# Small-head softmax: scores masked in place in PSUM, exponentials read from there, and their sums in the same banks

## The chip, the cores and the metric

The kernel is one program on one core of a Trainium2 chip. Five engines work side by side, each with its own queue in order: TensorE (PE; its weight loads are shown as PEld), VectorE (DVE), ScalarE (ACT), GpSimd (POOL), and SyncE (SP), which issues DMAs. The metric is the device time of one execution in microseconds; lower is better. PSUM has eight banks of 512 fp32 columns for each of 128 partitions, and matmul results land there.

## What is computed

The model is a stack of layers on x of shape [16, 256, 128] in float32: a mixture of experts, a causal attention with 16 heads of 8 channels, the mixture again, two layers of local attention with gated FFN, a retention layer, and the local layers again. The change lies in the causal attention, which reads in short:

```python
h = _layernorm(x)                       # [16, 256, 128]
q, k, v = split(h @ w_attn + b_attn)    # 16 heads, D = 8
q, k = _rope(q), _rope(k)
att = einsum('bhqd,bhkd->bhqk', q, k) / sqrt(D)
att = where(causal, att, -inf)
att = softmax(att, axis=-1)
y = einsum('bhqk,bhkd->bhqd', att, v)
x = x + y @ w_proj + b_proj
```

## The kernel before

The attention is the stage `small_head_softmax`. A batch is 256 tokens, two tiles t of 128 queries. Queries of tile 0 see 128 keys, those of tile 1 see 256, so one head has 128 + 256 = 384 score columns (`TRI`). A step s handles two heads (h = 0, 1); a batch b has `EACH` = 8 steps, e = 0 to 7, and the stage has U = 16 x 8 = 128 steps. Each head of a step has a PSUM bank of its own, and steps alternate between two pairs: banks 2 and 3 when e is even, 4 and 5 when it is odd.

A step's work goes through the engines like this:
- PE, L936: S, the score matmuls into the pair of banks. L957: transposes of the probabilities of step s-3 into banks 6 and 7. L975, on odd steps: the product with the values for two steps, into bank 1.
- DVE, L1108: four `tensor_tensor_reduce` (t by h). Each reads scores from PSUM, adds the causal mask `tri_q`, writes the masked scores to `pr` in SBUF and the negated row maximum to `nm`. It also reads an accumulator out, a short second row in the trace. L1117: reciprocal of the row sums of step s-1. L1124: copies the transposed probabilities of head 0 from bank 6 to SBUF (step s-3).
- ACT, L1053: four exponentials on `pr`, in place in SBUF, with `nm` as bias; the row sums go to `ls` in SBUF. L1069: the copy of head 1 from bank 7.
- POOL, L1008: multiplies `pr` by the reciprocals.

`pr` has four slots (`SLOTS`), used in turn. Beside this runs the preparation of the next batch: projection and bias (PE L911 at e = 0, ACT L1031), values (PE L918 at e = 4, ACT L1041), rotation on DVE (L1079 `cosines` at e = 1, L1082 `swap` at e = 2, L1086 `sines` at e = 3), its sum on POOL (`total`, L997, at e = 4), `queries` on DVE (L1092, at e = 5, 6, 7 and 0), and POOL's `carry` (L990). ACT L1062 writes the finished batch out at e = 4.

There is no scheduler: the order on each engine is the written order of the loop body, 14 of 16 batches run in a hardware loop of two batches, and the engines meet only at semaphores. Those that matter here: `s_ready` (scores there), `nm_ready` (maxima there), `p_ready` (exponentials done), `rl_ready` (reciprocals done), `normed`, `pt_ready` (transposes done), `pt_low` and `pt_high` (their copies done). S of step s waits for `nm_ready` of s-2, the last reader of its banks.

Of the kernel before, what the change touches and what calls it, by code (L numbers as in the profile page):

```python
# [10 lines left out]
ACT = mybir.ActivationFunctionType  # L11
# [4 lines left out]
B, T = 16, 256  # L16
N = B * T
MASKED = -1e30
FAR = 1e25
# [85 lines left out]
def at_least(u, n):  # L105

    return not isinstance(u, int) or u >= n
# [756 lines left out]
TRI = 384  # L864


def small_head_softmax(nc, g, sem, room, w, tab, bias, prev, room_free):

    U = B * EACH
    SLOTS = 4  # L870
    head_ps, ol = g.bank[0], g.bank[1][:, 0:T]
    s_ps = ((g.bank[2], g.bank[3]), (g.bank[4], g.bank[5]))
    pt_ps = (g.bank[6], g.bank[7])
    hT, xb, turn, qk, qz, vm, nm, ls, rl, pr = (room[x] for x in ("hT", "xb", "turn", "qk", "qz", "vm", "nm", "ls", "rl", "pr"))
    pt = g.z[:, 0:SLOTS * 2 * TRI].rearrange("p (s h n) -> p s h n", s=SLOTS, h=2)
    t1, t2 = (g.z[:, 8 * TRI + n * 2 * T:8 * TRI + (n + 1) * 2 * T] for n in range(2))
    names = ("v_zero", "h_ready", "proj_ready", "xb_ready", "vp_ready", "v_ready", "swapped", "turned", "qk_ready", "qz_ready",
# [23 lines left out]
    def tensor(pe):  # L901
        def project(b):
            if at_least(b, 1):
                pe.wait_ge(v_ready, b)
            if is_first(b):
                prev.there(pe, 0)
                prev.free(pe, 0)
            if isinstance(b, int) and b == 1:
                prev.there(pe, B // 2 - 1)
            for n in range(2):  # L910
                ins = mm(head_ps[:, n * T:(n + 1) * T], w[:, n, :], tokens(g.hn, b), start=(n == 0), stop=(n == 1), skip_group_check=True)  # L911
            ins.then_inc(proj_ready, 1)

        def values(b):
            pe.wait_ge(h_ready, b + 1)
            pe.wait_ge(xb_ready, b + 1)
            for t in range(2):
                ins = mm(head_ps[:, t * P:(t + 1) * P], hT[:, t * P:(t + 1) * P], w[:, 2, :], start=(t == 0), stop=(t == 1), skip_group_check=True)  # L918
            ins.then_inc(vp_ready, 1)

        def body(i):
            for s, b, k, e in steps(i):
                if runs(s, U):
                    jj, bank = e // 2, s_ps[e % 2]
                    if e % 2 == 0:
                        pe.wait_ge(qz_ready, 4 * b + jj + 1)
                    if isinstance(s, int) and s < 2:
                        prev.free(pe, 2 + 2 * s)
                        prev.free(pe, 3 + 2 * s)
                    if at_least(s, 2):  # L930
                        pe.wait_ge(nm_ready, s - 1)
                    for t, cols in ((0, slice(0, P)), (1, slice(P, TRI))):
                        for n in range(2):
                            q = 2 * (e % 2) + n
                            r = slice(32 * q, 32 * q + 32)
                            ins = mm(bank[n][:, cols], qz[r, k, jj, t * P:(t + 1) * P], qk[r, k, T:T + (t + 1) * P], start=(t == 0), stop=(t == 1), skip_group_check=True)  # L936
                    ins.then_inc(s_ready, 1)

                if runs(b + 1, B):
                    if e == 0:  # L940
                        project(b + 1)
                    if e == 4:
                        values(b + 1)

                u = s - 3
                if runs(u, U):
                    kk, ee = place(k, e, 3)
                    pe.wait_ge(normed, u + 1)
                    if is_first(u):
                        prev.free(pe, 6)  # L950
                        prev.free(pe, 7)
                    if at_least(u, 1):
                        pe.wait_ge(pt_low, u)
                        pe.wait_ge(pt_high, u)
                    for h in range(2):
                        for c in range(3):
                            ins = nc.tensor.transpose(pt_ps[h][:, c * P:(c + 1) * P], pr[:, ee % SLOTS, h, c * P:(c + 1) * P], g.ident32)  # L957
                    ins.then_inc(pt_ready, 1)

                u = s - 5  # L960
                if e % 2 and runs(u, U):
                    kk, ee = place(k, e, 5)
                    jj = ee // 2
                    pe.wait_ge(pt_low, u + 2)
                    pe.wait_ge(pt_high, u + 2)
                    if ee == 0:
                        pe.wait_ge(v_ready, b + 1)
                        if is_first(u):
                            prev.free(pe, 1)
                        if at_least(b, 1):  # L970
                            pe.wait_ge(out_ready, b)
                    for q0, col, n, kt in ((0, 0, T, 0), (P, T, P, 1)):
                        for q in range(4):
                            cs = slice(32 * q, 32 * q + 32)
                            ins = mm(ol[cs, q0:q0 + n], vm[:, kk, kt, jj * P + 32 * q:jj * P + 32 * q + 32], pt[:, (ee + q // 2) % SLOTS, q % 2, col:col + n],  # L975
                                     start=(jj == 0 and kt == 0), stop=(jj == 3 and kt == 1), skip_group_check=True)
                    ins.then_inc(pv_ready, 1)
        project(0)
        values(0)
        rounds(pe, 1, B // 2 - 1, 2, body)  # L980
# [41 lines left out]
    def scalar(act):  # L1022
# [21 lines left out]
        def body(i):  # L1044
            for s, b, k, e in steps(i):
                u = s - 1
                if runs(u, U):
                    kk, ee = place(k, e, 1)
                    act.wait_ge(nm_ready, u + 1)
                    for t, (c0, c1) in enumerate(((0, P), (P, TRI))):  # L1050
                        for h in range(2):
                            x = pr[:, ee % SLOTS, h, c0:c1]
                            ins = act.activation(x, x, ACT.Exp, scale=-1.0, bias=nm[:, ee % 2, t, h:h + 1], accum_out=ls[:, ee % 2, t, h:h + 1])  # L1053
                    ins.then_inc(p_ready, 1)
                if runs(b + 1, B):
                    if e == 0:
                        biased(b + 1)
                    if e == 5:
                        values(b + 1, 1 - k)
                if e == 4 and runs(b - 1, B):  # L1060
                    act.wait_ge(pv_ready, 4 * b)
                    act.activation(tokens(g.hn, b - 1), ol, ACT.Identity, bias=bias[:, 2:3]).then_inc(out_ready, 1)  # L1062
                u = s - 3
                if runs(u, U):
                    kk, ee = place(k, e, 3)
                    act.wait_ge(pt_ready, u + 1)
                    if at_least(u, 4):
                        act.wait_ge(pv_ready, 4 * of(b, e, 3) + ee // 2 - 1)
                    act.activation(pt[:, ee % SLOTS, 1, :], pt_ps[1][:, 0:TRI], ACT.Copy).then_inc(pt_high, 1)  # L1069
# [4 lines left out]
    def vector(dve):  # L1074
# [19 lines left out]
        def body(i):  # L1094
            for s, b, k, e in steps(i):
                if runs(s, U):
                    if not isinstance(s, int):
                        for n in (-1, 1, 3):
                            dve.compute_val(s - n)
                    dve.wait_ge(v_zero, 1)  # L1100
                    dve.wait_ge(s_ready, s + 1)
                    if at_least(s, 2):
                        dve.wait_ge(p_ready, s - 1)
                    if at_least(s, 4):
                        dve.wait_ge(pt_ready, s - 3)
                    for t, (c0, c1) in enumerate(((0, P), (P, TRI))):
                        for h in range(2):
                            ins = dve.tensor_tensor_reduce(pr[:, e % SLOTS, h, c0:c1], s_ps[e % 2][h][:, c0:c1], g.tri_q[:, c0:c1], -1.0, FAR,  # L1108
                                                           ALU.add, ALU.min, nm[:, e % 2, t, h:h + 1])
                    ins.then_inc(nm_ready, 1)  # L1110
                u = s - 1
                if runs(u, U):
                    kk, ee = place(k, e, 1)
                    dve.wait_ge(p_ready, u + 1)
                    if at_least(u, 2):
                        dve.wait_ge(normed, u - 1)
                    dve.reciprocal(rl[:, ee % 2, :, :], ls[:, ee % 2, :, :]).then_inc(rl_ready, 1)  # L1117
                u = s - 3
                if runs(u, U):
                    kk, ee = place(k, e, 3)  # L1120
# [23 lines left out]
        eng.wait_ge(out_ready, 2 * s + 2)  # L1144

    def free(eng, bank):
        last = ((turned, B), (out_ready, B), (nm_ready, U), (nm_ready, U), (nm_ready, U), (nm_ready, U), (pt_low, U), (pt_high, U))
        eng.wait_ge(*last[bank])

    return Stage(sync=nothing, tensor=tensor, scalar=scalar, vector=vector, gpsimd=gpsimd, there=there, free=free)  # L1150
# [912 lines left out]
```

## Time and profile before

| | us |
|---|---|
| three runs | 2301.33, 2302.54, 2312.95 |
| median | 2302.54 |
| profiled execution | 2294.92 |
| its span | 2293.1 |

| engine | busy us | share of the span |
|---|---|---|
| PE | 2136.7 | 93% |
| ACT | 1801.0 | 79% |
| DVE | 1706.8 | 74% |
| POOL | 1431.8 | 62% |

The span runs from the first to the last instruction of the profiled execution. The shares are averages over stages that differ. The changed stage lies between about 211 us (first L1108 at 210.9) and 528 us (last L1053 at 526.8), some 315 us of the span. Times in timelines count from the start of the span, and a duration includes the time in which an instruction's end overlaps the next one's start. So the distance between two starts (the pitch) tells what an instruction costs its engine, and the duration tells when its result is there.

### The profile page before, as it was taken

The numbers are of one execution on the slowest core, as the hardware profiler recorded it, in microseconds if no ns is written. First come the engines' busy times: TensorE is split into PE (matmuls) and PEld (weight loads), VectorE is DVE, ScalarE is ACT, GpSimd is POOL, SyncE is SP. The second block draws the span as 40 slices with busy tenths as digits, with TensorE's granted clock in tenths as the row PEclk, the third lists the DMA queues.
The fourth block names the chain that finished last, engine by engine and source line by source line (L and its number), as shares of the span: only waits on it lengthen the run. The fifth ranks groups of instructions, "written<-read, shape, count | busy, mean of one in ns | idle before, by whom it ended". The sixth has DMA issues, their size and how long they took to land. (4 is left out here: it accounts for less than half of the span.)

```text
span 2293.1 us, 67424 instructions
## 1 busy us (share of the span) xinstructions
PE 2136.7 (93%) x22342; PEld 1585.6 (69%) x22342; DVE 1706.8 (74%) x4362; ACT 1801.0 (79%) x6112; POOL 1431.8 (62%) x1432
## 2 busy tenths in 40 slices
PE   6997999998797999999999999898999999999999
PEld 4994666665795888854888854674788864788863
DVE  5565999996555899964899964675899963899964
ACT  4775999995676999973999973556999982999982
POOL 3663777774662888840888850671788850788850
PEclk8997999999899999999999999999999999999999
DMA  6111000000113000000000000000000000000000
GB/s 249 44 42 42 2 0 0 0 1 38 35 44 111 12 7 9 7 3 3 11 7 9 7 0 0 2 0 6 9 9 8 8 1 5 9 9 7 9 1 37
DMA packets 22568, 46.02 MB, mean 20 GB/s; under 512 B 5344, under 2 KB 13664, under 8 KB 22048
## 3 DMA queue, kind: packets, MB, share of 16 engines
q1 hardware_dynamic: 17440, 34.07, 4.4%
q0 software_dynamic: 4992, 10.23, 1.6%
q8 instruction: 73, 1.20, 0.2%
q14 instruction: 63, 0.52, 0.1%
HBM read 24.51 MB, written 11.40 MB: 16 GB/s over the span
## 5 line engine op out<-in xcount | busy, mean ns | idle before, releaser
L280 POOL TENSOR_TENSOR space<-space 128x512 f32<-128x512 f32 x256 | 325.8, 1273 | 270.4 <-DVE space L383 270.1
L275 POOL TENSOR_TENSOR space<-space 128x512 f32<-128x512 f32 x256 | 267.6, 1045 | 128.1 <-ACT space L316 127.6
L330 ACT ACTIVATE space<-psum,space 128x128 f32<-128x128 f32 x1024 | 337.0, 385 | 2.7 <-DVE space L374 2.7
L177 PE MATMUL psum<-big,space 128*128 128x256 f32 x1024 | 267.9, 384 | 7.3 <-issue 3.5
L269 POOL TENSOR_TENSOR space<-space 128x512 f32<-128x512 f32 x256 | 267.0, 1043 | 7.9 <-DVE space L354 7.3
L1008 POOL TENSOR_TENSOR space<-space 128x256 f32<-128x256 f32 (+1 forms) x256 | 221.9, 888 | 75.2 <-DVE space L1117 70.9
L374 DVE TENSOR_REDUCE space<-psum 128x4 f32<-128x512 f32 x256 | 177.1, 692 | 100.8 <-PE psum L192 96.5
L1053 ACT ACTIVATE space<-space 128x128 f32<-128x128 f32 (+1 forms) x512 | 226.1, 446 | 7.3 <-DVE space L1108 6.5
L330 ACT ACTIVATION_READ_ACCUMULATOR space<-psum,space 128x1 f32 x1024 | 201.8, 197 | 0.0
L177 PEld LDWEIGHTS psum<-big,space 128*128 128x128 f32 x1024 | 175.6, 191 | 29.6 <-issue 16.2
L677 ACT ACTIVATE big<-psum,wt 128x512 f32<-128x512 f32 (+1 forms) x96 | 65.4, 686 | 151.9 <-PE psum L654 151.9
L209 PE MATMUL psum<-space 64*64 64x128 f32 (+2 forms) x4096 | 174.7, 275 | 7.0 <-ACT space L301 7.0
L221 PE MATMUL psum<-space,big 128*128 128x256 f32 x512 | 179.0, 431 | 0.0
L255 PE MATMUL psum<-cf,space 128*128 128x128 f32 x1024 | 168.2, 287 | 11.5 <-POOL space L275 10.8
L381 DVE TENSOR_TENSOR space<-psum,tabs 128x512 f32<-128x512 f32 x256 | 174.4, 681 | 4.2 <-ACT space L306 3.9
L192 PE MATMUL psum<-space 64*64 64x64 f32 (+1 forms) x5120 | 171.8, 249 | 2.9 <-ACT space L295 2.9
L383 DVE TENSOR_TENSOR space<-psum,tabs 128x512 f32<-128x512 f32 x256 | 174.4, 681 | 0.0
L192 PEld LDWEIGHTS psum<-space 64*64 64x64 f32 x5120 | 110.6, 134 | 89.7 <-issue 89.7
L360 DVE CAST psum<-cb 128x512 f32<-128x512 bf16 x256 | 172.7, 674 | 0.0
L366 DVE TENSOR_REDUCE space<-space 128x8 f32<-128x512 f32 x256 | 171.6, 670 | 0.0
L654 PE MATMUL psum<-hn,big 128*128 128x512 f32 (+1 forms) x384 | 169.7, 592 | 0.0
L295 ACT ACTIVATE space<-psum 128x512 f32<-128x512 f32 x256 | 153.2, 599 | 16.0 <-PE psum L255 6.6
(194 smaller groups left out, 5425.8 us busy)
## 6 DMA issues: line engine op xcount, KB each, us to landing
big<-early SPq DMA_DIRECT2D x1, 6944.0 KB, 27.9
rows<-space SPq DMA_DIRECT2D x16, 256.0 KB, 2.7
z<-token_y SPq DMA_DIRECT2D x16, 256.0 KB, 4.7
space<-z SPq DMA_DIRECT2D x64, 64.0 KB, 1.9
space<-z SPq DMA_DIRECT2D x64, 63.8 KB, 2.1
big<-late SPq DMA_DIRECT2D x1, 3114.0 KB, 13.7
x<-x_t SPq DMA_DIRECT2D x4, 512.0 KB, 6.0
x_final<-x SPq DMA_DIRECT2D x8, 256.0 KB, 2.0
```

The costliest lines, as they stand in the source:

```text
L177: ins = mm(qk_ps[:, t * T:(t + 1) * T].rearrange("p (n c) -> p n c", n=2), hT[:, k, t * P:(t + 1) * P], wq[:, 0:2, j, :], start=(t == 0), ...
L192: ins = mm(s_ps[h][w * WIN:(w + 1) * WIN, col:col + n], qk[r, j % 2, q0:q0 + WIN], qk[r, j % 2, T + k0:T + k0 + n], start=False, stop=True ...
L209: ins = mm(ol[r][h * LD:(h + 1) * LD, q0:q0 + n], v[rows, j, tile, h * LD:(h + 1) * LD], pt[rows, j % 2, h, q0:q0 + n], start=(q0 == 0), s ...
L221: mm(z_ps, wo[:, c, :], oT[:, (j - 5) % 2, :], start=(c == 0), stop=(c == CH - 1), skip_group_check=True).then_inc(wo_ready, 1)
L269: pool.tensor_tensor(x, x, rl[:, (j - 3) % 2, :, :].rearrange("p h t -> p (h t)").unsqueeze(2).to_broadcast([P, 4, P]), ALU.mult).then_inc ...
L275: pool.tensor_tensor(x, x, rn[:, (j - 1) % 2, :].unsqueeze(2).to_broadcast([P, 8, LD]), ALU.mult).then_inc(scaled, 1)
L280: pool.tensor_tensor(t3[:, j % 2, :], t1[:, j % 2, :], t2[:, j % 2, :], ALU.add).then_inc(summed, 1)
L330: ins = act.activation(pr[:, j % 2, h, t * P:(t + 1) * P], s_ps[h][:, t * P:(t + 1) * P], ACT.Exp, bias=nm[:, j % 2, h, t:t + 1], accum_ou ...
L374: dve.tensor_reduce(nm[:, j % 2, :, :], s_pair.rearrange("p h (t n) -> p h t n", t=2), AX.X, ALU.max, negate=True).then_inc(nm_ready, 1)
L381: dve.tensor_tensor(t1[:, j % 2, :], qk_ps, tab[:, 0, :], ALU.mult)
L1008: ins = pool.tensor_tensor(x, x, rl[:, ee % 2, t, :].unsqueeze(2).to_broadcast([P, 2, c1 - c0]), ALU.mult)
L1053: ins = act.activation(x, x, ACT.Exp, scale=-1.0, bias=nm[:, ee % 2, t, h:h + 1], accum_out=ls[:, ee % 2, t, h:h + 1])
```

## The change

- L1108 writes the masked scores back into the score banks instead of `pr`.
- The exponentials read the banks and write `pr`. Their sums go to two columns of the same banks behind the 384 score columns (`ls`), and the reciprocal reads them there.
- S waits for `rl_ready` of step s-2 instead of `nm_ready` of s-2.
- The wait for a free slot of `pr` (`pt_ready` of s-4) moves from DVE to ACT. What the later stages wait for to take banks 2 to 5 is `rl_ready` as well.

```diff
     s_ps = ((g.bank[2], g.bank[3]), (g.bank[4], g.bank[5]))
+    ls = tuple(x[:, :, TRI:TRI + 2] for x in (g.bank_pair2, g.bank_pair4))
...
                     if at_least(s, 2):
-                        pe.wait_ge(nm_ready, s - 1)
+                        pe.wait_ge(rl_ready, s - 1)
...
                     act.wait_ge(nm_ready, u + 1)
+                    if at_least(u, 4):
+                        act.wait_ge(pt_ready, u - 3)
                     for t, (c0, c1) in enumerate(((0, P), (P, TRI))):
                         for h in range(2):
-                            x = pr[:, ee % SLOTS, h, c0:c1]
-                            ins = act.activation(x, x, ACT.Exp, scale=-1.0, bias=nm[:, ee % 2, t, h:h + 1], accum_out=ls[:, ee % 2, t, h:h + 1])
+                            ins = act.activation(pr[:, ee % SLOTS, h, c0:c1], s_ps[ee % 2][h][:, c0:c1], ACT.Exp, scale=-1.0,
+                                                 bias=nm[:, ee % 2, t, h:h + 1], accum_out=ls[ee % 2][:, h, t:t + 1])
                     ins.then_inc(p_ready, 1)
...
-                    if at_least(s, 4):
-                        dve.wait_ge(pt_ready, s - 3)
                     for t, (c0, c1) in enumerate(((0, P), (P, TRI))):
                         for h in range(2):
-                            ins = dve.tensor_tensor_reduce(pr[:, e % SLOTS, h, c0:c1], s_ps[e % 2][h][:, c0:c1], g.tri_q[:, c0:c1], -1.0, FAR,
+                            ins = dve.tensor_tensor_reduce(s_ps[e % 2][h][:, c0:c1], s_ps[e % 2][h][:, c0:c1], g.tri_q[:, c0:c1], -1.0, FAR,
...
-                    dve.reciprocal(rl[:, ee % 2, :, :], ls[:, ee % 2, :, :]).then_inc(rl_ready, 1)
+                    dve.reciprocal(rl[:, ee % 2, :, :], ls[ee % 2].rearrange("p h t -> p t h")).then_inc(rl_ready, 1)
...
-        last = ((turned, B), (out_ready, B), (nm_ready, U), (nm_ready, U), (nm_ready, U), (nm_ready, U), (pt_low, U), (pt_high, U))
+        last = ((turned, B), (out_ready, B), (rl_ready, U), (rl_ready, U), (rl_ready, U), (rl_ready, U), (pt_low, U), (pt_high, U))
```

No instruction moves on any engine; operands and waits change. On PE, in the loop at e = 1 of a batch, stood before (the semaphores carry the stage's prefix `ss_`, and line numbers are those of each kernel's own text):

```order
L936 MATMUL psum<-space 128x128 [waits ss_nm_ready]
L936 MATMUL psum<-space 128x128
L936 MATMUL psum<-space 128x256 x2
L957 MATMUL psum<-cf,space 128x128 [waits ss_pt_high,ss_pt_low,ss_normed]
L957 MATMUL psum<-cf,space 128x128 x5
L975 MATMUL psum<-z,space 32x256 [waits ss_pt_high,ss_pt_low]
```

and stands now:

```order
L937 MATMUL psum<-space 128x128 [waits ss_rl_ready]
L937 MATMUL psum<-space 128x128
L937 MATMUL psum<-space 128x256 x2
L958 MATMUL psum<-cf,space 128x128 [waits ss_pt_high,ss_pt_low,ss_normed]
L958 MATMUL psum<-cf,space 128x128 x5
L976 MATMUL psum<-z,space 32x256 [waits ss_pt_high,ss_pt_low]
```

S stands where it stood, ahead of the transposes and the values product, and waits for another event. On DVE, a step of the loop (e = 3) stood before:

```order
L1108 ISA space<-psum,cb 128x128 [waits ss_p_ready,ss_pt_ready,ss_s_ready,ss_v_zero]
L1108 ISA space 128x1
L1108 ISA space<-psum,cb 128x128
L1108 ISA space 128x1
L1108 ISA space<-psum,cb 128x256
L1108 ISA space 128x1
L1108 ISA space<-psum,cb 128x256
L1108 ISA space 128x1
L1117 RECIPROCAL space<-space 128x4 [waits ss_normed,ss_p_ready]
L1124 COPY z<-psum 128x384 [waits ss_pv_ready,ss_pt_ready]
```

and stands now:

```order
L1109 ISA psum,space<-psum,cb 128x128 [waits ss_p_ready,ss_s_ready,ss_v_zero]
L1109 ISA space 128x1
L1109 ISA psum,space<-psum,cb 128x128
L1109 ISA space 128x1
L1109 ISA psum,space<-psum,cb 128x256
L1109 ISA space 128x1
L1109 ISA psum,space<-psum,cb 128x256
L1109 ISA space 128x1
L1118 RECIPROCAL space<-psum 128x4 [waits ss_normed,ss_p_ready]
L1125 COPY z<-psum 128x384 [waits ss_pv_ready,ss_pt_ready]
```

The reciprocal that S of the next step now waits for is the one behind these four pairs of rows, which belong to a step later than it.

## Rows read from the trace of the kernel before

**Rows 1.** Windows: stretch, length, busy PE, PEld, DVE, ACT, POOL (instructions), PE clock, DMA.

```profile
300.00:400.00 100.00, 91.42 (x945) 61.95 (x945) 92.83 (x451) 96.22 (x392) 78.50 (x92) 1.00 0.00 0
```

**Rows 2.** Timeline, ACT: start, duration (us), engine, line, operation, operands.

```profile
400.05 0.39 ACT L1053 ACTIVATE space<-space 128x128 f32<-128x128 f32 x1
...
400.44 0.49 ACT L1053 ACTIVATE space<-space 128x256 f32<-128x256 f32 x1
...
400.93 0.49 ACT L1053 ACTIVATE space<-space 128x256 f32<-128x256 f32 x1
```

**Rows 3.** Timeline, DVE, one batch from e = 4.

```profile
341.78 0.28 DVE L1108 CUSTOM_DVE_ANT_0 space<-psum,cb 128x128 f32<-128x128 f32 x1
...
343.67 0.29 DVE L1108 CUSTOM_DVE_ANT_0 space<-psum,cb 128x128 f32<-128x128 f32 x1 [0.16 <-issue]
...
346.11 0.79 DVE L1092 TENSOR_SCALAR space<-space,cf 128x256 f32<-128x256 f32 x1 [0.50 <-PE psum L936]
346.83 0.28 DVE L1108 CUSTOM_DVE_ANT_0 space<-psum,cb 128x128 f32<-128x128 f32 x1
...
347.03 0.28 DVE L1108 CUSTOM_DVE_ANT_0 space<-psum,cb 128x128 f32<-128x128 f32 x1
...
347.25 0.41 DVE L1108 CUSTOM_DVE_ANT_0 space<-psum,cb 128x256 f32<-128x256 f32 x1
...
347.59 0.41 DVE L1108 CUSTOM_DVE_ANT_0 space<-psum,cb 128x256 f32<-128x256 f32 x1
...
347.94 0.17 DVE L1117 RECIPROCAL space<-space 128x4 f32<-128x4 f32 x1
...
348.87 0.28 DVE L1108 CUSTOM_DVE_ANT_0 space<-psum,cb 128x128 f32<-128x128 f32 x1
...
351.28 0.29 DVE L1108 CUSTOM_DVE_ANT_0 space<-psum,cb 128x128 f32<-128x128 f32 x1 [0.30 <-issue]
...
352.89 0.56 DVE L1124 COPY z<-psum 128x384 f32<-128x384 f32 x1 [0.32 <-PE psum L957]
...
354.33 0.28 DVE L1108 CUSTOM_DVE_ANT_0 space<-psum,cb 128x128 f32<-128x128 f32 x1
...
356.77 0.28 DVE L1108 CUSTOM_DVE_ANT_0 space<-psum,cb 128x128 f32<-128x128 f32 x1
...
359.05 0.27 DVE L1108 CUSTOM_DVE_ANT_0 space<-psum,cb 128x128 f32<-128x128 f32 x1
...
361.48 0.28 DVE L1108 CUSTOM_DVE_ANT_0 space<-psum,cb 128x128 f32<-128x128 f32 x1
```

**Rows 4.** Timeline, PE, from e = 7 to e = 0.

```profile
348.65 0.85 PE L957 MATMUL psum<-cf,space 128*128 128x128 f32 x6 [0.90 <-DVE z L1124]
...
350.21 0.92 PE L936 MATMUL psum<-space 32*128 32x128 f32 x8
```

**Rows 5.** Timeline, a stalled S behind DVE.

```profile
215.09 0.42 DVE L1108 CUSTOM_DVE_ANT_0 space<-psum,cb 128x256 f32<-128x256 f32 x1
...
215.57 0.92 PE L936 MATMUL psum<-space 32*128 32x128 f32 x8 [1.40 <-DVE space L1108]
```

**Rows 6.** Timeline, POOL, at e = 4.

```profile
343.14 1.61 POOL L1008 TENSOR_TENSOR space<-space 128x256 f32<-128x256 f32 x2 [0.38 <-DVE space L1117]
344.71 1.27 POOL L997 TENSOR_TENSOR space<-z 128x512 f32<-128x512 f32 x1
```

**Rows 7.** Timeline, ACT, local attention.

```profile
1099.77 0.39 ACT L330 ACTIVATE space<-psum,space 128x128 f32<-128x128 f32 x1
...
1100.07 0.41 ACT L330 ACTIVATE space<-psum,space 128x128 f32<-128x128 f32 x1
```

**Rows 8.** Timeline, DVE, local attention.

```profile
1100.68 0.68 DVE L360 CAST psum<-cb 128x512 f32<-128x512 bf16 x1
1101.26 0.67 DVE L366 TENSOR_REDUCE space<-space 128x8 f32<-128x512 f32 x1
```

**Rows 9.** Timeline, DVE, end of the stage.

```profile
527.45 0.18 DVE L1117 RECIPROCAL space<-space 128x4 f32<-128x4 f32 x1 [1.49 <-ACT space L1053]
```

More of the change, by code:

```diff
@@ L872, in small_head_softmax @@
     s_ps = ((g.bank[2], g.bank[3]), (g.bank[4], g.bank[5]))
+    ls = tuple(x[:, :, TRI:TRI + 2] for x in (g.bank_pair2, g.bank_pair4))
     pt_ps = (g.bank[6], g.bank[7])
-    hT, xb, turn, qk, qz, vm, nm, ls, rl, pr = (room[x] for x in ("hT", "xb", "turn", "qk", "qz", "vm", "nm", "ls", "rl", "pr"))
+    hT, xb, turn, qk, qz, vm, nm, rl, pr = (room[x] for x in ("hT", "xb", "turn", "qk", "qz", "vm", "nm", "rl", "pr"))
     pt = g.z[:, 0:SLOTS * 2 * TRI].rearrange("p (s h n) -> p s h n", s=SLOTS, h=2)
@@ L1097, in body @@
                     if not isinstance(s, int):
-                        for n in (-1, 1, 3):
+                        for n in (-1, 1):
                             dve.compute_val(s - n)
```

## The prediction

> **What bounds the kernel now.** I read the page first and then only one stage. The diff touches `small_head_softmax` alone, about 315 of 2293 us, so no gain there can be large for the whole. The view by windows comes next: in a steady stretch of that stage ACT is busy 96.2 of 100 us, DVE 92.8, PE 91.4, POOL 78.5, and TensorE has its full clock, 2.4 GHz [rows 1]. ACT looks like the bound, but the others are close behind, so I ask what sets each step.
>
> The timeline of DVE answers that. The stage has 128 steps (16 batches of 8 head pairs); I call a step by its place e = 0 to 7 in its batch, and measure it from the first L1108 of one step to the first of the next. One batch reads, from e = 4: 1.89, 3.16, 2.04, 2.41, 3.05 (this one is e = 0), 2.44, 2.28, 2.43, together 19.70 us, or 2.46 a step [rows 3]. Who sets them? 3.16 at e = 5: `queries` (L1092) waits until 346.11 for POOL's `total` (L997), which ends at 344.71 + 1.27 [rows 3, 6]. (The row names PE's L936, but the scores that `queries` waits for are a batch old; `total` ended 0.13 before.) 3.05 at e = 0: L1124 stands at 352.89 behind PE's transposes, which themselves wait behind the next batch's projection [rows 3]. 2.41 at e = 7: PE has transposes from 348.65, then the values product, S from 350.21, and DVE starts 1.07 later [rows 3, 4]. The short steps, 1.89 and 2.04, are DVE's own queue. So ACT is nearly full, yet not the only limit.
>
> **What the change takes from ACT.** Now one exponential of 128 columns starts 0.39 after another and a 256-column one holds ACT 0.49 [rows 2]: 2 x 0.39 + 2 x 0.49 = 1.76 us a step. L330 in the other attention already has the new form (reads PSUM, its sum goes to PSUM): 128 columns every 0.30 us [rows 7]. That is 0.09 less for each instruction, and since the columns cost the same in both, I take 0.09 for the 256-column ones too. 4 x 0.09 = 0.36 us a step, 128 x 0.36 = 46 us of ACT's time. The new wait of ACT for the transposes of four steps before (`pt_ready`) is free: they run on PE two steps ahead of that exponential. DVE loses the same wait, which is not seen in its rows either.
>
> **What it adds: a ring.** The score banks are held longer. S of step s+1 waited for the maxima of s-1; now it waits for the reciprocal of s-1 (`rl_ready`), because the masked scores and the sums live in the banks until then. That reciprocal stands in DVE's queue behind the four L1108 of step s, and these need S of step s. So the ring S(s), L1108(s), reciprocal(s-1), S(s+1) has to close once in every step:
> - S start to first L1108: 351.28 - 350.21 = 1.07 us [rows 3, 4].
> - first L1108 to reciprocal: 347.94 - 346.83 = 1.11 [rows 3].
> - the reciprocal itself: 0.17 [rows 3].
> - DVE's end to PE's start: L1108 ends at 215.09 + 0.42 = 215.51, PE starts at 215.57: 0.06 [rows 5].
>
> Sum: 2.41 us, a floor for every step. It doesn't matter that ACT is 0.36 faster: the exponential of s-1 has a whole step to finish, and in the ring only its reciprocal counts. PE's own chain at odd steps, transposes and values from 348.65 to 350.21, is 1.56, and an S of 0.92, less the 0.07 by which it overlaps the next, makes it 2.41 as well [rows 4]; the two agree and do not add. What is queued behind PE's new wait are the transposes of s-2 and the values; with the wait over at the floor they come in time, since DVE copies only after its reciprocal.
>
> **Step by step with that floor.**
> - e = 1, 2.44: stays, DVE's queue is longer than the ring.
> - e = 2, 2.28: 2.41, +0.13.
> - e = 3, 2.43: stays.
> - e = 4 and 5, 1.89 + 3.16 = 5.05: stays. The fourth becomes 2.41, but the pair is set by reciprocal, POOL's multiply at 343.14, `total` at 344.71, `queries` at 346.11 and the next L1108 at 346.83, all counted from the start of step 4 [rows 3, 6]; the fifth shrinks by as much.
> - e = 6, 2.04: 2.41, +0.37.
> - e = 7, 2.41: 2.43, as S of the next batch meets ring and PE chain together, +0.02.
> - e = 0, 3.05: stays, it is counted from S by PE's queue.
>
> That is +0.52 a batch; the reciprocal, reading four sums from PSUM, I give 0.01 more in four ring steps: +0.54. For 14 inner batches 7.6 us. The first batch has S(2) issued early now and will have it wait for the first reciprocal, at a lower clock: I estimate +2. In the last batch the short steps lose some 0.35 a pair, but the end gets back what it waits for ACT now (1.49 at 527.45 [rows 9]): about +0.2. Sum +10 us. The profiled execution took 2294.9 (span 2293.1), so 2305 by its account; the median of the three runs is 2302.5, 7.6 above it, and I put the change on that: 2312.
>
> **The unknown: L1108 writing PSUM.** No instruction of before reads and writes PSUM on DVE. The nearest that writes it, L360, takes 0.68 us for 512 columns and the next DVE instruction starts 0.58 after it. (In L1108 the starts are 0.21 apart for 128 columns and 0.34 for 256 [rows 3], so 128 columns cost 0.13 and 512 of them 0.53.) L366, which neither reads nor writes PSUM, takes 0.67 [rows 8]. So a PSUM output costs nothing visible: I take 0 per instruction. The ends: it may save up to 0.05 us, what L360's pitch has over its columns, or, if reading and writing one bank share its port, double the columns: 768 more in a step, 0.8 us. Each 0.01 us on the four instructions is 0.04 a step, about 5 us in all, since they stand in DVE's queue and in the ring.
>
> A rule speaks against the change here. The Trainium skill, page "Perfetto Trace Analysis", section "Optimizing Scalar/DVE Operations", gives VectorE an overhead of about 60 ns an instruction on SBUF and about 125 on PSUM. If this counted for an output on top of an input in PSUM, the estimate from the page would be 65 ns x 4 x 128 = 33 us more. L360 against L366 [rows 8] doesn't show it, but L360's input is in SBUF. The same result is rival 2, worked out from rows.
>
> **Rivals.**
> 1. *ACT was the bound and the ring is slack* (faster). For: ACT's 96.2% [rows 1] and its 0.36 a step. The kernel would come down to DVE's own queue, which is 92.8 of 100 us busy: 2.46 x 0.93 = 2.29 a step, -0.17 x 128 = -22, with the ends about -20: 2283. Against: the ring is a chain of waits in the code and its four pieces are measured. It decides only if the pieces shrink: with 0.05 us less in each L1108 the ring is 2.21, and the net is 10 - 128 x 0.20 = -16 us, 2287. Chance 0.12.
> 2. *The in-place write costs about as much again as the access that can be seen*: L1108 has 0.21 from start to start for 128 columns (0.13 of columns, so 0.08 of overhead); with 0.06 more in each, 0.24 a step in ring and queue alike, +31 on top of the 10: 2343. Place: L1108 on DVE. It decides from 0.02 us each (2322). For: nothing in the trace has both sides in PSUM. Against: rows 8. Chance 0.15.
> 3. *Half rate in place*: +0.8 x 128 = +102: about 2415. Chance 0.04.
> 4. *The PSUM output is cheaper than the SBUF output, by 0.02 us in each L1108*: 0.08 a step in ring and queue, 128 x 0.08 = 10 us, all that the ring costs: 2302. For: L360's 0.05 over its columns against 0.08 in L1108. Against: L1108 also reads its maximum out, which L360 does not. Chance 0.19.
>
> The forecast itself has 0.50, with 2304 to 2321 as its own range.
>
> **Numbers.** What a measurement can tell from no change is 0.5%, 11.5 us, and my +10 lies close to it. Faster: rival 1 and a little of 4, 0.13. Slower: rivals 2 and 3 (0.19) and less than half of the forecast (0.23), 0.42. The same: 0.45. The range leaves out rival 3, most of rival 1's far half and the upper part of rival 2: 2287 to 2345.
>
> **What would show it.** Right: L1053's successor at pitch 0.30 and 0.40 with ACT busy some 80 to 85 of 100 us; no step from L1108 to L1108 under 2.4; PE idle before S waiting for DVE's reciprocal; e = 6 grown by 0.37, the pair 4 + 5 unchanged; batch 20.2. Wrong: L1108 at another pitch than 0.21 and 0.34 (rivals 1 to 3), steps under 2.4 (the ring isn't there), or a batch longer though L1108 is the same (a wait I don't see, in POOL's chain or behind PE's new one).

## The result, and the profile after

The kernel became slower: 2339.56 us (median of four runs, 2337.07 to 2343.26) against 2303.85 (four runs of the kernel before), a ratio of 1.0149, interval 1.0118 to 1.0180. The forecast said +10 us and the medians show +35.7, so it was too small by 26. The time lies inside the range of 2287 to 2345, in its upper part, but outside the 2304 to 2321 that the forecast gave as its own. The profiled execution took 2343.26 (span 2341.5).

| us | before | after |
|---|---|---|
| span | 2293.1 | 2341.5 |
| ACT busy | 1801.0 | 1777.5 |
| DVE busy | 1706.8 | 1725.3 |
| the stage, from the first step's first L1108 (L1109) to the last step's first | 312.9 | 347.5 |
| mean granted PE clock, whole span | 0.978 | 0.97 |

The stage explains 34.6 us, nearly all that the medians show (35.7). The spans differ by 48.4, but the rest lies outside: the changed stage starts at 219.18 instead of 210.95, in code that is the same, and some 6 us come behind it. I leave those out: the profiled execution of before, 2294.92, is faster than all its other runs, and that of after, 2343.26, the slowest of its four.

The same stretch as [rows 1], in the windows view of the kernel after, and below it four windows from around 320 us (length, then busy PE, PEld, DVE, ACT and POOL, granted PE clock, DMA):

```profile
300.00:400.00 100.00, 88.01 (x856) 58.33 (x848) 89.23 (x409) 81.71 (x357) 71.92 (x84) 0.97 0.00 0
...
316.00:318.00 2.00, 1.73 (x14) 1.16 (x14) 2.00 (x9) 1.73 (x9) 1.88 (x2) 1.00 0.00 0
318.00:320.00 2.00, 1.34 (x9) 0.70 (x10) 1.69 (x8) 1.76 (x9) 1.84 (x4) 0.78 0.00 0
320.00:322.00 2.00, 2.00 (x14) 1.38 (x18) 1.90 (x11) 0.69 (x4) 0.76 (x2) 0.50 0.00 0
322.00:324.00 2.00, 2.00 (x24) 1.20 (x17) 0.95 (x5) 1.85 (x9) 1.59 (x2) 0.87 0.00 0
```

ACT fell from 96.2 to 81.7 and all other engines fell with it: something between them sets the pace, and it isn't the engine that was relieved. The small windows show what no batch of the kernel before has behind the first one: PE idles, the granted clock goes from 2.4 to 1.2 GHz (0.50), PE is busy without a gap, and DVE and ACT get less to do. There are four such falls, at 319, 384, 469 and 555 us, in batches that are some 1.4 us longer than their neighbours (22.48, 22.44 and 22.43 against 21.02, and one in the last batch).

The timeline of DVE and PE around one ring, the answer to [rows 3 and 4]:

```profile
349.94 0.29 DVE L1109 CUSTOM_DVE_ANT_0 psum<-psum,cb 128x128 f32<-128x128 f32 x1
...
350.14 0.33 DVE L1109 CUSTOM_DVE_ANT_0 psum<-psum,cb 128x128 f32<-128x128 f32 x1
...
350.39 0.46 DVE L1109 CUSTOM_DVE_ANT_0 psum<-psum,cb 128x256 f32<-128x256 f32 x1
...
350.77 0.46 DVE L1109 CUSTOM_DVE_ANT_0 psum<-psum,cb 128x256 f32<-128x256 f32 x1
...
351.16 0.17 DVE L1118 RECIPROCAL space<-psum 128x4 f32<-128x4 f32 x1
...
352.45 0.30 DVE L1109 CUSTOM_DVE_ANT_0 psum<-psum,cb 128x128 f32<-128x128 f32 x1 [0.28 <-issue]
...
353.68 0.18 DVE L1118 RECIPROCAL space<-psum 128x4 f32<-128x4 f32 x1
```

```profile
351.38 0.92 PE L937 MATMUL psum<-space 32*128 32x128 f32 x8 [0.91 <-DVE space L1118]
...
353.91 0.92 PE L937 MATMUL psum<-space 32*128 32x128 f32 x8
```

The reciprocal at 351.16 ends at 351.33, S starts at 351.38; DVE starts at 352.45, 1.07 later; its reciprocal comes 1.23 after that, at 353.68, and S follows at 353.91. One turn is 2.53 us, and DVE itself waits in it (the 0.28 that the row puts down to issue). L1109 starts 0.20, 0.25, 0.38 and 0.39 after one another, where L1108 had 0.20, 0.22, 0.34 and 0.35 [rows 3].

Steps of an inner batch, from one first L1108 (L1109) to the next:

| | e=0 | 1 | 2 | 3 | 4 | 5 | 6 | 7 | batch |
|---|---|---|---|---|---|---|---|---|---|
| before | 3.05 | 2.44 | 2.28 | 2.43 | 1.89 | 3.16 | 2.04 | 2.41 | 19.70 |
| after | 3.17 | 2.55 | 2.52 | 2.57 | 2.52 | 2.64 | 2.52 | 2.53 | 21.02 |

The waits between 300 and 400 us (engine, its line, what it waited for: us, times, longest), then ACT's exponentials, the answer to [rows 2], and the end of the stage, the answer to [rows 9]:

```profile
PEld psum L937 <- DVE space L1118: 20.7, 36, 1.1
PE psum L937 <- DVE space L1118: 11.8, 18, 0.9
```

```profile
300.11 0.37 ACT L1055 ACTIVATE space<-psum,space 128x128 f32<-128x128 f32 x1
...
300.43 0.37 ACT L1055 ACTIVATE space<-psum,space 128x128 f32<-128x128 f32 x1
...
300.73 0.49 ACT L1055 ACTIVATE space<-psum,space 128x256 f32<-128x256 f32 x1
...
301.13 0.51 ACT L1055 ACTIVATE space<-psum,space 128x256 f32<-128x256 f32 x1
```

```profile
569.68 0.18 DVE L1118 RECIPROCAL space<-psum 128x4 f32<-128x4 f32 x1 [1.19 <-ACT space L1055]
```

S waits for the reciprocal in nearly every step of the stretch. The pitch of an exponential is 0.30 to 0.32 and 0.40, as forecast. The last reciprocal still waits 1.19 us for ACT, where the whole wait of 1.49 was expected to come back. It starts 3.04 us after the last step's first L1109 (566.64), where that was 3.60 before, so 0.56 us came back.

### The profile page after: what moved, and what is told of

It reads as the page before. It is cut to its first block and busy times, and to the rows that moved or that the text cites. A ratio compares the mean times of both kernels' runs of the same rounds, so it can differ in the third digit from the quotient of the medians.

```text
span 2341.5 us, 67424 instructions
## 1 busy us (share of the span) xinstructions
PE 2158.9 (92%) x22342; PEld 1597.0 (68%) x22342; DVE 1725.3 (74%) x4362; ACT 1777.5 (76%) x6112; POOL 1430.5 (61%) x1432
## 5 line engine op out<-in xcount | busy, mean ns | idle before, releaser
L1055 ACT ACTIVATE space<-psum,space 128x128 f32<-128x128 f32 (+1 forms) x512 | 196.6, 440 | 22.9 <-DVE space L1109 20.1
L1109 DVE CUSTOM_DVE_ANT_0 psum<-psum,cb 128x128 f32<-128x128 f32 (+1 forms) x512 | 167.4, 387 | 40.3 <-issue 33.7
L360 DVE CAST psum<-cb 128x512 f32<-128x512 bf16 x256 | 172.5, 674 | 0.0
L937 PE MATMUL psum<-space 32*128 32x128 f32 (+1 forms) x1024 | 125.1, 364 | 48.3 <-DVE space L1118 43.9
```

Of the source, the lines that this page charges most:

```text
L1055: ins = act.activation(pr[:, ee % SLOTS, h, c0:c1], s_ps[ee % 2][h][:, c0:c1], ACT.Exp, scale=-1.0, bias=nm[:, ee % 2, t, h:h + 1], accum_ ...
```

## The experiments

The runs came in three groups, each with its own chip allocation and its own runs of the kernel before: wait_only, psum_out_only, exp_raw and sums_sbuf (median of before 2304.83), then recip_mid, busy_pe, shared_sums and shared_total (2275.39), then the rest (2303.37). A ratio is to the kernel before of the same group, and total times of different groups are not compared. Lengths of batches and of the stage are: the kernel after has the same in two groups (347.5 and 347.6, see changed_again). The two things that the change does on DVE and PE were taken apart first.

### wait_only: the kernel before with only the later wait of S

```diff
-                        pe.wait_ge(nm_ready, s - 1)
+                        pe.wait_ge(rl_ready, s - 1)
```
(and the same semaphore in `free`, here and in the other edits where it belongs to the wait)

> The kernel before, with only S waiting for the reciprocal (rl_ready of s-2) instead of the maxima. Ring theory: the ring S, four L1108, reciprocal, S closes at 2.41 us, no step is shorter, an inner batch takes 20.2 us against 19.70, stage +9, whole +10 us. Clock theory (PE idle before S lets the granted clock fall to 1.2 GHz): on top of it a longer slow start and some stretches of about 4 us at the lower clock, each +1.4, together +15 to +20 us. If instead the in-place write is the whole cause of the slowdown: batch 19.70, no change.

Measured: 2320.50, ratio 1.0073 (1.0060 to 1.0086). The batch takes 20.24 (3.05, 2.44, 2.40, 2.45, 2.41, 2.65, 2.40, 2.45). PE in its timeline:

```profile
346.96 0.92 PE L936 MATMUL psum<-space 32*128 32x128 f32 x8 [0.35 <-DVE space L1117]
...
349.40 0.92 PE L936 MATMUL psum<-space 32*128 32x128 f32 x8 [0.71 <-DVE space L1117]
```

The two S are 2.44 apart and both wait for the reciprocal. So the ring exists and costs 0.54 us a batch by itself. The stage is 328.5 long, +15.6, and not +10: the inner batches give 7.6, the first batch takes 26.07 where it took 22.21, the last steps 17.12 (15.05), and one batch is 1.6 longer through a fall of the clock. That is the outcome which the expectation's clock theory gives (+15 to +20), and not the ring theory alone.

### psum_out_only: the kernel before with L1108 writing the banks

```diff
-ins = dve.tensor_tensor_reduce(pr[:, e % SLOTS, h, c0:c1], s_ps[...][:, c0:c1], g.tri_q[:, c0:c1], ...)
+ins = dve.tensor_tensor_reduce(s_ps[e % 2][h][:, c0:c1], s_ps[...][:, c0:c1], g.tri_q[:, c0:c1], ...)
```

> The kernel before, with only L1108 writing back into the score banks; waits as before. The exponentials still read pr, which nothing masks or fills, so the scores don't reach the softmax. Write theory (each in-place L1108 costs 0.03 us more from start to start, 0.12 a step): DVE is the bound of most steps, so an inner batch takes 19.70 + 6 or 7 x 0.12 = 20.4 to 20.5, whole +11 to +13 us. Ring theory alone: batch 19.70, no change. Pitch of L1108 0.22 to 0.25 and 0.38 either way, if the cost is the output and not ACT's use of the same banks; 0.21 and 0.34 if it is the latter.

This kernel leaves the scores out of the softmax: its exponentials read `pr`, which nothing fills. Measured: 2318.41, ratio 1.0063 (1.0050 to 1.0076); batch 20.40, stage 324.1. Groups of instructions between 300 and 400 us (count, busy us and mean ns of one, idle before them), of this kernel and then of before:

```profile
L1108 DVE CUSTOM_DVE_ANT_0 psum<-psum,cb 128x256 f32<-128x256 f32 x78 | 32.9, 461 | 0.0
...
L1108 DVE DVE_READ_ACCUMULATOR2_ANT space<- 128x1 f32 x156 | 21.3, 137 | 0.0
```

```profile
L1108 DVE CUSTOM_DVE_ANT_0 space<-psum,cb 128x256 f32<-128x256 f32 x82 | 31.2, 416 | 0.0
...
L1108 DVE DVE_READ_ACCUMULATOR2_ANT space<- 128x1 f32 x164 | 13.0, 79 | 0.0
```

The output in PSUM costs by itself 0.70 us a batch. The durations grow by 45 ns, and the row that reads the accumulator out by 58, but most of that overlaps the next instruction: the starts move apart by 0.12 in a step of four, 0.03 us each. sums_sbuf below, which leaves nothing out, has the same batch of 20.40.

### exp_raw: the kernel after with L1109 writing `pr`, outside PSUM

```diff
-ins = dve.tensor_tensor_reduce(s_ps[e % 2][h][:, c0:c1], s_ps[...][:, c0:c1], ...)
+ins = dve.tensor_tensor_reduce(pr[:, e % SLOTS, h, c0:c1], s_ps[...][:, c0:c1], ...)
```

(and DVE's wait for a free slot of `pr` is back in its place)

> The changed kernel, with L1108 writing pr in SBUF again, while the exponentials still read the score banks (the mask does not reach them). Ring and ACT's speed stay, the in-place write goes. Ring theory: steps of 2.41, batch 20.2, the same as with the wait alone, although ACT is 0.36 us a step faster; 0.8 a batch or 12 us below the changed kernel. If ACT's exponentials on PSUM were what slows DVE: L1108 stays at 0.38 for 256 columns and the batch at 21.0.

This kernel leaves the mask out: the exponentials read the raw scores. Measured: 2324.39, ratio 1.0082 (1.0069 to 1.0095); batch 20.27, stage 333.2. In the same view:

```profile
L1111 DVE CUSTOM_DVE_ANT_0 space<-psum,cb 128x256 f32<-128x256 f32 x80 | 30.5, 417 | 0.0
...
L1111 DVE DVE_READ_ACCUMULATOR2_ANT space<- 128x1 f32 x159 | 12.8, 81 | 0.0
```

With the exponentials fast (ACT busy 86.6 of 100 us) and the DVE output back in SBUF, the batch is that of wait_only, 20.27 and 20.24. This shows both that ACT's gain is worth nothing here and that 0.75 of the 1.32 us a batch came through the output. The 0.03 over wait_only lie where the forecast had put 0.04 for a reciprocal that reads PSUM, but no run separates them from the exponentials' new form. One long stretch at 1.2 GHz, 514 to 528 us, makes one batch 26.19.

### sums_sbuf: the kernel after with the sums in SBUF, S waiting for ACT

```diff
-                        pe.wait_ge(rl_ready, s - 1)
+                        pe.wait_ge(p_ready, s - 1)
...
-..., accum_out=ls[ee % 2][:, h, t:t + 1])
+..., accum_out=ls[:, ee % 2, t, h:h + 1])
```

> The changed kernel with the row sums in SBUF, so that S can wait for the exponentials (p_ready of s-2) and not for the reciprocal. The ring through DVE's queue is gone. Ring theory: PE doesn't wait for the reciprocal, steps e = 6 and e = 4 fall below 2.41 again, but each step keeps the 0.12 of the in-place write: batch 3.17 + 2.56 + 2.40 + 2.56 + 5.16 + 2.16 + 2.41 = 20.4 against 21.0, and fewer clock falls, together -12 to -18 us against the changed kernel, +10 to +15 above the kernel before. Rival (the slowdown is all in-place write): batch stays 21.0.

Measured: 2321.24, ratio 1.0073 (1.0059 to 1.0086); batch 20.40, the same as psum_out_only, so the ring is gone and the output's price left. Here too ACT is faster and the batch is not: ACT is busy 89.3 of 100 us, against 93.3 in psum_out_only. ACT in its timeline:

```profile
346.19 0.38 ACT L1054 ACTIVATE space<-psum,space 128x128 f32<-128x128 f32 x1
...
346.54 0.38 ACT L1054 ACTIVATE space<-psum,space 128x128 f32<-128x128 f32 x1
...
346.88 0.50 ACT L1054 ACTIVATE space<-psum,space 128x256 f32<-128x256 f32 x1
...
347.33 0.50 ACT L1054 ACTIVATE space<-psum,space 128x256 f32<-128x256 f32 x1
```

The pitch is 0.35 and 0.45, half way between 0.39 and 0.49 [rows 2] and 0.30 and 0.40 after. Of the 0.09 that an exponential saves, half is the source in PSUM and half the sum in PSUM. Its stage, at 329.4, is 5.3 longer than that of psum_out_only, with a first batch at 1.2 GHz from 209 to 244 us.

### busy_pe: the kernel after with three more transposes on even steps

```diff
-                    for h in range(2):
-                        for c in range(3):
+                    for h, c in [(h, c) for h in range(2) for c in range(3)] + ([(1, c) for c in range(3)] if e % 2 == 0 and e else []):
```

> The changed kernel with three transposes of each step e = 2, 4, 6 issued once more (same input, same output), 0.4 us of PE work where it waits for the ring. Clock theory: PE is idle less in front of S, so the falls to 1.2 GHz in mid-stage (4 in the profile of the changed kernel, 1.4 us each) become 0 or 1 and the batch stays at 21.0: -3 to -8 us in all. Rival (the falls have nothing to do with PE's idle time): still 3 to 5 falls, no gain. If PE were what bounds these steps, the batch would grow by 3 x 0.4 = 1.2 us, +18.

Measured: 2305.29, ratio 1.0125 (1.0108 to 1.0142).

```profile
300.00:400.00 100.00, 92.01 (x923) 62.80 (x920) 92.77 (x420) 83.78 (x369) 74.79 (x87) 1.00 0.00 0
```

No fall of the clock is left inside the stage, the batch stays at 21.02, and the stage is 340.0 long, 7.5 less than after. Other kernels of this group do show falls (recip_mid seven, shared_sums one), so it is not the group that lacks them. Filling PE's idle time thus went with the loss of all four falls, in one profiled execution.

The share of time in which PE is busy does not explain them by itself. psum_out_only has the same share as the kernel after, and no fall between its first batch and its last L1108:

```profile
300.00:400.00 100.00, 88.00 (x896) 59.53 (x893) 94.29 (x431) 93.30 (x379) 76.03 (x89) 1.00 0.00 0
```

Nor does the wait for the reciprocal: in wait_only S waits for it 10.7 us of 100, against 11.8 in the kernel after, and the clock falls once and not four times; and shared_sums, without that wait and with PE busy 91.1, has one fall too. What decides where a fall comes stays open. What the falls cost in the whole time isn't resolved either: 1.0125 and 1.0149 have intervals that overlap, and the kernel after itself did not run in this group.

### recip_mid: the kernel after with the reciprocal between the two tiles' L1109

```diff
+                    masks(0)
                     dve.reciprocal(rl[...], ls[ee % 2].rearrange("p h t -> p t h")).then_inc(rl_ready, 1)
+                    masks(1).then_inc(nm_ready, 1)
```
(`masks(t)` holds the two L1109 of tile t)

> The changed kernel with the reciprocal of s-1 issued between the second and the third L1108 of step s; sums stay in PSUM and S still waits for rl_ready. Ring theory: the ring shrinks from 2.52 to 1.07 + 0.47 + 0.18 + 0.06 = 1.8 us and no longer sets a step, so DVE's queue does: batch 20.4 as in sums_sbuf, -10 to -15 us against the changed kernel. Rival (holding the banks longer is the cost, wherever the reciprocal stands): batch 21.0. If the reciprocal now waits for the exponential in DVE's queue, up to 20.8.

Measured: 2322.92, ratio 1.0202 (1.0184 to 1.0220), the highest of all. Inner batches take 21.8 to 22.5, but for one of 25.11 with the clock down from 261 to 272 us; some 58 us of the stage are at 1.2 GHz. In the timeline of DVE and POOL:

```profile
347.92 0.18 DVE L1121 RECIPROCAL space<-psum 128x4 f32<-128x4 f32 x1 [0.16 <-ACT space L1055]
...
348.18 1.61 POOL L1009 TENSOR_TENSOR space<-space 128x256 f32<-128x256 f32 x2 [1.08 <-DVE space L1121]
...
349.19 1.14 DVE L1082 TENSOR_TENSOR z<-space,cf 128x512 f32<-128x512 f32 x1
```

The theory forgot what stands behind the reciprocal. DVE now waits for ACT in the middle of its group and the maxima come later, so ACT waits 17.6 us of 100 for them. POOL's multiply, released earlier, has run for 1.0 us when DVE's `cosines` start, and these take 1.14 us; in the kernel after it had run for 0.29, and `cosines` took 0.87 while POOL's two instructions took 2.06 instead of 1.61. My expectation was wrong here.

### shared_sums: sums_sbuf with ACT taking four of eight head-0 copies

```diff
+                    if e in (0, 1, 3, 5):
+                        act.activation(pt[:, ee % SLOTS, 0, :], pt_ps[0][:, 0:TRI], ACT.Copy).then_inc(pt_low, 1)
```
(and DVE leaves these out)

> sums_sbuf with the copy of head 0 from bank 6 moved from DVE to ACT at e = 0, 1, 3, 5. DVE theory (with the ring gone DVE's queue is the bound and ACT's gain lies idle): DVE loses 0.44 at these steps, ACT has room for 0.37; e = 0 goes from 3.17 to about 2.6 (PE then), e = 1 and 3 from 2.56 to 2.1, the pair 4 and 5 stays near 5.1 behind POOL: batch 18.9, -24 us against sums_sbuf, -12 us against the kernel before. Rival (ACT, with two copies in a row, becomes late for the exponentials): batch 19.7 or more, no gain over the kernel before.

Measured: 2288.02, ratio 1.0056 (1.0040 to 1.0071). Batch 19.75 to 19.91, and one of 21.41 with a fall of the clock at 444 us; stage 319.2. ACT's free time has a use after all: the batch is 0.5 to 0.65 shorter than sums_sbuf's. But it isn't the 18.9 that I expected. The rival was right: ACT, busy 97.4 of 100 us with DVE at 84.1, is late, and S waits for its exponentials 6.8 us of 100.

### shared_total: the same with `total` first on POOL at e = 4

```diff
+                if e == 4 and runs(b + 1, B):
+                    total(b + 1, 1 - k)
                 u = s - 1
```
(and not behind the multiply any more)

> shared_sums, and on POOL at e = 4 the sum total of the next batch (1.27 us) goes ahead of the multiply instead of behind it. It then ends before queries (DVE, e = 5) asks for it, so the pair of steps 4 and 5 goes from 5.1 to about 4.3: batch 18.1, another -12 us, or -25 us against the kernel before. Bound then: PE, 17.7 us of work a batch. Rival: POOL's multiply is late for the transposes, batch 18.9 as in shared_sums.

Measured: 2282.64, ratio 1.0031 (1.0021 to 1.0042); batch 19.66 to 19.72, stage 315.1.

```profile
300.00:400.00 100.00, 91.81 (x946) 61.94 (x939) 86.29 (x427) 97.71 (x414) 78.63 (x93) 1.00 0.00 0
```

The expected 18.1 was missed by 1.6, and the kernel is still behind the one before. ACT is full now; with one copy less on it the batch falls to 19.3 (shared3_total below).

### changed_again: the kernel after once more

> The changed kernel itself, on the chip of this group, as the control that the last group lacked. Inner batches 21.0 again. Against the kernel before +33 to +40 us as on the first chip if the granted clock falls in mid-stage as often; with 0 falls some 6 less.

Measured: 2334.81, ratio 1.0126 (1.0098 to 1.0154), batch 21.02, stage 347.6. The falls of the clock come in the same four batches, at 316, 381, 466 and 551 us, where the first profile has them at 319, 384, 469 and 555 (its stage starts about 3 us later). They belong to the kernel and are no accident of one execution.

### before_total: the kernel before with `total` first on POOL

The diff is that of shared_total.

> The kernel before with only POOL's total ahead of the multiply at e = 4. POOL theory: the pair of steps 4 and 5 (5.05 us) no longer waits for total; DVE's own queue wants 1.66 + 2.1 there, ACT's work allows 18.9 a batch at least: batch 19.2 to 19.5, -3 to -8 us. Rival (ACT, 96% busy, is the bound and the pair only collects its lag): batch 19.7, no change.

Measured: 2296.05, ratio 0.9971 (0.9956 to 0.9986). Batch 19.22, stage 306.4.

```profile
300.00:400.00 100.00, 93.11 (x958) 63.22 (x956) 94.27 (x460) 97.91 (x401) 80.86 (x95) 1.00 0.00 0
```

```profile
344.75 1.27 POOL L997 TENSOR_TENSOR space<-z 128x512 f32<-128x512 f32 x1
...
346.27 3.23 POOL L1010 TENSOR_TENSOR space<-space 128x256 f32<-128x256 f32 x4 [0.25 <-POOL space L997]
...
347.57 0.47 DVE L1092 TENSOR_SCALAR space<-space,cf 128x256 f32<-128x256 f32 x1
```

`total` no longer stands behind the multiply [rows 6], the first `queries` do not wait for it and take 0.47 and not 0.79, and the steps e = 4 and 5 shrink from 5.05 to 4.46. ACT's work is what it was (97.9 of 100 us busy) and the batch is 0.48 shorter all the same, so ACT's 96% did not bound the kernel before. This kernel beats both, by a little: some 7 us.

### shared3_total and shared2_total: shared_total with three and two copies on ACT

`e in (0, 1, 3)` and `e in (0, 3)` in place of `(0, 1, 3, 5)`.

> shared_total with the head 0 copy on ACT only at e = 0, 1, 3. There ACT was busy 97.7% with four such copies and DVE 86%. Balance theory: one copy less takes 0.37 from ACT, batch 19.3 to 19.4 against 19.7, -5 us against shared_total, about the kernel before. Rival (the steps are set by waits between the engines, not by ACT's load): batch 19.7.

> shared_total with the copy on ACT only at e = 0 and 3. ACT's work falls to 18.5 a batch, DVE's rises to 17.9; the step e = 1 with the cosines is 2.56 again. Balance theory: batch 19.1 to 19.4, -5 to -9 us against shared_total and a little under the kernel before. Rival: 19.7 or more.

Measured: 2303.70, ratio 1.0001 (0.9987 to 1.0015), and 2304.91, 0.9995 (0.9980 to 1.0010). Batches of 19.29 to 19.37 in both, ACT busy 98.2 and 95.8, against 19.22 in before_total. The balance theory's batch came true for both, but taking the third copy away gained nothing more. With the load spread as well as I could, exponentials from PSUM bring the kernel back to where it was and no further; against before_total, which has the same order on POOL, they are still 8 and 9 us behind. As I read it, DVE pays for the output what ACT gains; no run separates the two there.

## Why the prediction was right, and where its size was off

**The direction and the mechanism held.** ACT's 46 us were worth nothing (exp_raw). The ring is there, its pieces were S to L1108 1.07, the reciprocal 0.17 to 0.18, back to PE 0.05: all as forecast. Alone it costs 0.54 a batch (wait_only), by the steps foreseen: e = 2 +0.12, e = 6 +0.36, e = 7 +0.04, and e = 4 and 5 together 5.06 against 5.05. The forecast had 0.52 for it, and 0.04 on top for a reciprocal that this kernel does not have; that both come to 0.54 is chance.

**That the time lies in the range is in part luck.** The range reached to 2345 for the lower part of rival 2, and it is that part which came true, with costs of the clock on top that no rival held. By its own sign of being wrong, "L1108 at another pitch than 0.21 and 0.34", the forecast's zero for the output fails.

**Mis-sized: "a PSUM output costs nothing visible: I take 0 per instruction".** It costs 0.03 us in each (psum_out_only, exp_raw), 0.11 to 0.12 in the ring's second piece (1.11 forecast, 1.23 measured). The table of steps shows it cleanly: take the forecast's gains off the step differences (0.13 from e = 2, 0.37 from e = 6, 0.02 from e = 7) and 0.10 to 0.14 is left in each of e = 0, 1, 2, 3, 6 and 7, and 0.11 in the pair. In 14 inner batches that is 0.78 x 14 = 11 us. It is rival 2 at half its price: 0.03 lies over the 0.02 from which the text let it decide. The cost was read off L360, which writes PSUM from SBUF and has no accumulator to read out; which of the two makes the difference, no run says. By the text's own rate of 5 us for each 0.01, 0.03 is some 15 us.

The Trainium skill, page "Perfetto Trace Analysis", section "Optimizing Scalar/DVE Operations", puts VectorE's overhead at 60 ns on SBUF and 125 on PSUM. The direction was right; the pitch here grew by 30 ns for an output beside an input in PSUM, half of the 65, while the accumulator's row grew by 58 (79 to 137 ns).

**Mis-sized: the ends, "I estimate +2" and "about +0.2".** The first batch grew by 7 us (22.21 to 29.16), since TensorE ran at 1.2 GHz from about 217 to 247 us where it had done so from 208 to 214 and from 217 to 228, with the full clock between; wait_only has part of this too (26.07). The last steps took 19.42 and not 15.05: 1.4 a clock fall, 0.9 the output, 2.1 the ring. Of the wait of [rows 9], which was to come back whole, 1.19 stayed; counted from the last step's first L1109, 0.56 came back.

**Not foreseen: the clock inside the stage.** "PE idle before S waiting for DVE's reciprocal" stood in the text as a sign, but not that the granted clock might fall. Four falls at some 1.4 us are 5.7 us.

Together: ring 7.6 + 2.1, output 11 + 0.9, first batch 7, falls 5.7, sum 34.3, against 34.6 in the stage. The two halves run alone give less, 15.6 (wait_only) and 11.2 (psum_out_only), 26.8 together; most of the rest lies in the falls (some 4 us more than in wait_only) and in the first batch (2). Behind the split is a caution: why the first batch stays at 1.2 GHz for longer was not tried by itself. sums_sbuf has no wait for the reciprocal and shows 35 us of it, so the ring alone does not explain it; and shared3_total and shared2_total, which differ by one copy a batch, have first batches of 21.91 and 27.64. That stays open.

**The other rivals.** Rival 1 (ACT the bound) falls with wait_only, exp_raw and before_total, rival 3 (half rate) and rival 4 (output cheaper) with L1109's pitch.

## What to carry to other kernels

Relieving an engine that is 96% busy may be worth nothing: look at whether its neighbours' queues and a ring of waits close at the same length, and cost the ring before the instruction. Writing a result back into the bank it came from lengthens the time that the bank is held, by everything that stands ahead of the releasing instruction in its queue. And where TensorE gets a small wait in every step, check its granted clock: here falls of the clock cost 5.7 us more, and kernels with nearly the same waits or the same idle share had none or one.

## What the runs showed of the hardware

- A DVE operation with both sides in PSUM and a row maximum read out: pitch 0.03 to 0.04 us more than with its output in SBUF, at 128 and at 256 columns alike (0.25 and 0.38 against 0.22 and 0.34); its duration 416 to 461 ns, the accumulator's row 79 to 137.
- An exponential with a sum: pitch 0.39 with everything in SBUF, 0.35 with its source in PSUM, 0.30 with source and sum there (128 columns).
- Inside the stage of the kernel after the granted clock falls to 1.2 GHz for some 4 us at four places, the same in two executions, each time close behind an idle time of TensorE of 0.8 us before S, which other batches have as well. With three more transposes on even steps (PE busy 92.0 of 100 us) there were none. But the busy share alone does not tell: 88.0 in the kernel after with four falls, 88.0 in psum_out_only with none.
- DVE and POOL slow each other where their `TENSOR_TENSOR` lie side by side, and which of them pays differs with their starts: `cosines` 0.69 us with POOL idle (in front of the stage), 0.87 beside POOL's two at 2.06, or 1.14 beside the same two at 1.61. `queries` mostly take 0.47, 0.79 or 1.04 in the kernel before; what decides between these was not tried.
